# A two-layer graph network on one core: loop with hand-written schedule against an unrolled order by lags

## The chip, the cores and the metric

One core of a Trainium2 chip (trn2) runs the whole program. The metric is the device time of that core in microseconds, the median of several runs.

## What is computed

For 64 graphs of 128 nodes with 128 features (float32) and an integer adjacency matrix of 0 and 1:

```python
e      = leaky_relu((x * a_0) @ x.T, 0.2)           # only adj == 1 occurs in the data
alpha  = softmax(where(adj == 1, e, -9e15), axis=-1)
y      = layernorm(x + alpha @ x)
h      = y @ W_loop.T ;  g = h @ Wg_loop.T
vals   = (h + b_loop) * sigmoid(g + bg_loop)
out    = layernorm(y + relu(adj.T @ vals))
```

Other values of `adj` would take a general path, which is in the program and is skipped here; a sum over `adj` at the end decides that. Sigmoid is written as tanh: 0.5·(tanh(z/2)+1).

## The kernel before, in words

Four graphs make a group, so there are 16 groups of 128 × 512 elements. Five engines each run a list of stages in a fixed order, and semaphores join them. In the order of the data one group g passes through these stages (line numbers in brackets):

- SyncE loads `xt`, `adj_s`, `x_s` of a group (L530 to L532) into one of four slots, and stores `out_s` (L550).
- ScalarE: `weigh` (xat = xt·a, L643), `absent` (1 − adj, with its sum by an accumulator, L631), `mask` (adj as float, L636).
- TensorE `products` (L809: a penalty where there is no edge, L813: the scores, into one of two halves of `p_e`); ScalarE `relu` (L647); VectorE `scores` (L733, four instructions and their maxima); ScalarE `exp` (L654, four, with their sums by an accumulator); TensorE `turn_probs` (L828); ScalarE `turned_probs` (L664); TensorE `attend` (L838); VectorE `inverse` (1/sum, L740), `residual1` (L749, four) and `stats1` (L756, two).
- GpSimd `norm1`: variance + eps (L592), its power −1/2 (L594), and y = res1 · rstd (L596), a 128×512 multiply. This y is not centred; the mean is taken out by centring the weights (`w_mid`).
- TensorE `turn_y` (L847); ScalarE `turned_y` (L668); TensorE `gate_a`, `gate_b`: per half group one bf16 matmul that lays the biases down (L858, operands `ones3` and `b_parts`) and two matmuls of 256 columns (L861); ScalarE `tanh` (L672); VectorE `values` (L762); TensorE `sum_a`, `sum_b` (L872); VectorE `residual2` (L774) and `stats2` (L781).
- GpSimd `norm2`: variance (L602), centring (L613), power −1/2 (L616), multiply into `out_s` (L621). For the last four groups ScalarE does the last step (`finish`, L683).

The table `SCHEDULE` gives each engine a head, a loop body of one turn per group (unrolled four times, in a hardware loop) and a tail. What matters for what follows is the distance between stages on two engines. In one turn of the body VectorE does `residual1:3 scores:4 stats1:3 residual2:1 stats2:1`: it takes the first statistics of a group, and the second ones of the group two before. GpSimd's body is `norm2:2 norm1:5`: the second norm of a group, then the first norm of the group three after. So when GpSimd comes to `norm2` of a group, its `stats2` ended a whole VectorE turn before the `stats1` that the following `norm1` needs.

A `wait_alone` is a wait followed by an instruction that only adds to a semaphore; it stands ahead of L592, L602 and L733.

Of the kernel before, what the change touches and what calls it, by code (L numbers as in the profile page):

```python
# [5 lines left out]
ALU = mybir.AluOpType  # L6
ACT = mybir.ActivationFunctionType
# [10 lines left out]
LATE = 4  # L18
# [8 lines left out]
UNROLL = 4  # L27

SCHEDULE = {
    "tensor": (3, """
        products:0 products:1 turn_probs:0 attend:0 products:2 turn_probs:1 attend:1 products:3 turn_probs:2
        turn_y:0 attend:2 gate_a:0 gate_b:0 turn_y:1 sum_a:0 sum_b:0 gate_a:1 gate_b:1
        """, """
        turn_probs:3 products:4 attend:3 turn_y:2 sum_a:1 sum_b:1 gate_b:2 gate_a:2
        """, """
        turn_probs:15 attend:15 sum_a:13 turn_y:14 sum_b:13 gate_a:14 gate_b:14 sum_a:14 turn_y:15 sum_b:14
        gate_a:15 gate_b:15 sum_a:15 sum_b:15
        """),  # L40
    "scalar": (3, """
        weigh:0 absent:0 relu:0 weigh:1 absent:1 exp:0 relu:1 turned_probs:0 weigh:2 absent:2 exp:1 relu:2
        turned_probs:1 weigh:3 absent:3 exp:2 relu:3 turned_probs:2 mask:0 turned_y:0 mask:1 tanh_a:0
        tanh_b:0 turned_y:1
        """, """
        weigh:4 exp:3 absent:4 turned_probs:3 tanh_b:1 tanh_a:1 mask:2 relu:4 turned_y:2
        """, """
        exp:15 turned_probs:15 tanh_a:13 mask:14 tanh_b:13 turned_y:14 finish:12 tanh_a:14 mask:15 tanh_b:14
        turned_y:15 finish:13 tanh_a:15 tanh_b:15 finish:14 finish:15
        """),  # L50
    "vector": (3, """
        scores:0 inverse:0 scores:1 residual1:0 stats1:0 inverse:1 scores:2 residual1:1 stats1:1
        inverse:2 scores:3 residual1:2 values_a:0 values_b:0 stats1:2 inverse:3
        residual2:0 stats2:0
        """, """
        values_b:1 values_a:1 residual1:3 scores:4 stats1:3 residual2:1 stats2:1 inverse:4
        """, """
        values_a:13 residual1:15 values_b:13 stats1:15 residual2:13 stats2:13 values_a:14 values_b:14 residual2:14 stats2:14 values_a:15 values_b:15 residual2:15
        stats2:15
        """),  # L60
    "gpsimd": (2, """
        norm1:0 norm1:1 norm1:2 norm2:0 norm1:3 norm2:1 norm1:4
        """, """
        norm2:2 norm1:5
        """, """
        norm2:10 norm1:13 norm2:11 norm1:14 norm2:12 norm1:15 norm2:13 norm2:14 norm2:15
        """),
# [3 lines left out]
def program(nc, x, x_t, adj, a_0, a_all, w, wg_t, b_loop, b_fwd, b_bwd, out):  # L71


# [7 lines left out]
    with ExitStack() as ctx:  # L81
# [12 lines left out]
        ones3 = sb("ones3", [3, P], BF16)  # L94
        ones_col = sb("ones_col", [P, 1])
        minus_half = sb("minus_half", [P, G])
        minus_one = sb("minus_one", [P, G])
# [8 lines left out]
        b_rows = sb("b_rows", [3, 2 * P])  # L106
        b_rest = sb("b_rest", [3, 2, 2 * P])
        b_part = sb("b_part", [3, 3, 2 * P], BF16)
        b_sum = sb("b_sum", [3, 2, 2 * P], BF16)
        b_parts = sb("b_parts", [3, 2, 2 * P], BF16)  # L110

        x_s = sb("x_s", [P, 4, G, P])
        adj_s = sb("adj_s", [P, 4, G, P], I32)
        mask = sb("mask", [P, 4, G, P])
        absent = sb("absent", [P, 2, G, P], BF16)


# [40 lines left out]
        x_loaded = [sem(f"x_loaded{i}") for i in range(4)]  # L158
        adj_loaded = [sem(f"adj_loaded{i}") for i in range(4)]
# [4 lines left out]
        b_step = sem("b_step")  # L164
# [6 lines left out]
        xt_loaded = [sem(f"xt_loaded{i}") for i in range(4)]  # L171
# [11 lines left out]
        pool1 = sem("pool1")  # L183
# [17 lines left out]

# [29 lines left out]
        g_bias = [sb(f"g_bias{d}", [P, n, 2 * P]) for d, n in enumerate(n_rel)]  # L231
# [58 lines left out]
        def general_sync(sp):  # L290
# [46 lines left out]
        def general_vector(dve):  # L337
            dve.wait_ge(general_known, 1)
            found = dve.value_load(general[0:1, 0:1], min_val=0, max_val=1)
            with dve.If(found > 0):  # L340
# [7 lines left out]
                with dve.Fori(0, n_graphs) as b:  # L348
# [10 lines left out]
                    nc.vector.tensor_copy(g_xt[:], p_e[:, 1, 0]).then_inc(g_xt_ready, 1)  # L359
                    nc.vector.tensor_copy(g_adjf[:, 1], p_e[:, 1, 1]).then_inc(g_xt_ready, 1)  # L360
# [6 lines left out]
                    nc.vector.tensor_scalar(g_fifth[:], p_e[:, 0], SLOPE, None, ALU.mult).then_inc(g_attn, 1)  # L367
                    own = 2 + 2 * KINDS + 1
                    dve.wait_ge(g_attn, own * b + 1)
                    nc.vector.tensor_tensor(g_leaky[:], p_e[:, 0], g_fifth[:], ALU.max).then_inc(g_attn, 1)  # L370
# [15 lines left out]
                    nc.vector.scalar_tensor_tensor(out=g_res[:], in0=p_o[:, 0], scalar=g_rz[:], in1=g_x[:],  # L386
# [43 lines left out]
        def general_tensor(pe):  # L430
            pe.wait_ge(general_known, 1)
            found = pe.value_load(general[0:1, 0:1], min_val=0, max_val=1)
            with pe.If(found > 0):
# [7 lines left out]
                with pe.Fori(0, n_graphs) as b:  # L441
                    pe.wait_ge(g_loaded, 32 * (b + 1))
                    nc.tensor.transpose(p_e[:, 1, 0], g_x[:], ident[:]).then_inc(g_turned, 1)
                    pe.wait_ge(g_adjf_ready, b + 1)
                    nc.tensor.transpose(p_e[:, 1, 1], g_adjf[:, 0], ident[:]).then_inc(g_turned, 1)
                    pe.wait_ge(g_xa_ready, KINDS * (b + 1))
                    for k in range(KINDS):
                        last = nc.tensor.matmul(p_e[:, 0, k], g_xa[:, k], g_xt[:], start=True, stop=True)
# [4 lines left out]
                    nc.tensor.matmul(p_o[:, 0], g_prob_t[:], g_x[:], start=True, stop=True).then_inc(g_attended, 1)  # L453
# [25 lines left out]
        def is_first(g, n=1):  # L479

            return isinstance(g, int) and g < n

        def is_late(g):

            return isinstance(g, int) and g >= n_groups - LATE

        def of_half(f, h):
            return lambda g, s: f(g, s, h)

        engines = {"tensor": nc.tensor, "scalar": nc.scalar, "vector": nc.vector, "gpsimd": nc.gpsimd}  # L490

        def run(eng, stages):

            turns, head, body, tail = SCHEDULE[eng]

            def do(name, turn=None):
                stage, group = name.split(":")
                g, f = int(group), stages[stage]
                if turn is None:
                    f(g, g % UNROLL)  # L500
                else:
                    f(turn * UNROLL + g, g % UNROLL)

            order = head.split(), body.split(), tail.split()
            names = [n.split(":")[0] for n in order[1]]
            assert sorted(names) == sorted(set(stages) - {"finish"})
            done = list(order[0])
            for name in order[0]:
                do(name)

# [404 lines left out]
```

## Time and profile before

| | us |
|---|---|
| median of 3 runs | 132.62 (131.41 to 133.52) |
| the profiled execution | 132.06 |
| its span, first to last instruction | 130.2 |
| outside the span | 1.86 |

Times in the rows are microseconds from the start of the span, unless ns is written. One f32 matmul leaves two records, and matmul ends are modelled. A duration includes the way through the engine; the next instruction may start some 0.1 us before it ends, so the time an instruction occupies its engine is read from one start to the next.

### The profile page before, as it was taken

Reading aid. Unit: us, or ns where it says so; the run is one execution under the profiler, and the core shown is the slowest. Engines: PE = TensorE matmul, PEld = TensorE weight load, DVE = VectorE, ACT = ScalarE, POOL = GpSimd, SP = SyncE. Lnnn points to the kernel's source line nnn. Section 1 sums busy time; section 2 is a strip of 40 time slices with the busy share of each in tenths; the row PEclk is TensorE's granted clock in tenths of the full one; section 3 lists DMA queues with packets and bytes.
Section 4 is the critical chain, followed back from the end, with each engine's and each line's share of the span. In section 5 each row is a group of like instructions: output and inputs, shape, how many; then the busy total and the mean of one; then the engine's idle time right before and its main releaser. Section 6 shows DMA issues by size and latency. Waiting matters only on the chain.

```text
span 130.2 us, 2906 instructions
## 1 busy us (share of the span) xinstructions
PE 114.8 (88%) x706; PEld 93.9 (72%) x713; DVE 82.9 (64%) x336; ACT 98.8 (76%) x308; POOL 81.4 (63%) x124
## 2 busy tenths in 40 slices
PE   6767778999999999999999999999999997799500
PEld 6757567678878787878787878787878784675400
DVE  0537286635868686868686868686868686756420
ACT  4437899586979797979797979797979785767622
POOL 4000035427678787978797979797979797493340
PEclk9999999999999999999999999999999999999995
DMA  2999500592082656455646465646464202020222
GB/s 54 307 292 290 146 0 0 151 282 61 0 261 61 167 160 182 143 153 172 184 138 181 141 173 149 190 134 189 133 189 133 81 0 81 5 83 0 81 81 83
DMA packets 34768, 17.28 MB, mean 133 GB/s; under 512 B 1219, under 2 KB 34758, under 8 KB 34758
## 3 DMA queue, kind: packets, MB, share of 16 engines
q1 hardware_dynamic: 34608, 17.17, 47.2%
q8 instruction: 3, 0.05, 0.2%
q14 instruction: 7, 0.06, 0.1%
q10 hardware_dynamic: 150, 0.00, 0.1%
HBM read 12.98 MB, written 4.19 MB: 132 GB/s over the span
## 4 chain that ended last, share of the span: by engine, by line
PE 79%; ACT 10%; DMA 3%; issue 3%; DVE 1%; ACTq 0%; SPq 0%; POOL 0%; POOLq 0%; DVEq 0%
PE p_hg L861 26%; PE p_e L813 12%; PE p_ag L872 11%; PE p_o L838 10%; PE p_hg L858 8%; PE p_ut L828 5%; PE p_yt L847 5%; DMA adj_s<-adj 3%; ACT prob L654 2%; ACT absent L631 2%; PE p_e L809 2%; ACT prob_t L664 2%; ACT xat L643 1%; ACT rel L647 1%; ACT out_s L683 1%
## 5 line engine op out<-in xcount | busy, mean ns | idle before, releaser
L861 PE MATMUL p_hg<-w_both,y_t 128*128 128x256 f32 x128 | 36.2, 405 | 0.0
L861 PEld LDWEIGHTS p_hg<-w_both,y_t 128*128 128x128 f32 x128 | 21.7, 189 | 8.9 <-issue 7.3
L762 DVE SCALAR_TENSOR_TENSOR vals<-th,p_hg 128x256 f32<-128x256 f32 x32 | 12.4, 418 | 20.1 <-ACT th L672 20.1
L654 ACT ACTIVATE prob<-nscore,nmax 128x128 f32<-128x128 f32 x64 | 24.7, 389 | 0.4 <-DVE nmax L733 0.4
L592 POOL TENSOR_SCALAR rs<-st 128x4 f32<-128x4 f32 x16 | 3.2, 197 | 33.6 <-DVE st L756 33.6
L749 DVE SCALAR_TENSOR_TENSOR res<-p_o,rz,x_s 128x128 f32<-128x128 f32 x64 | 18.0, 344 | 8.4 <-PE p_o L838 4.3
L838 PE MATMUL p_o<-x_s,prob_t 128*128 128x128 f32 x128 | 17.5, 280 | 2.3 <-ACT prob_t L664 2.3
L813 PE MATMUL p_e<-xt,xat 128*128 128x128 f32 x128 | 18.6, 292 | 0.7 <-ACT absent L631 0.4
L872 PE MATMUL p_ag<-vals,mask 128*128 128x128 f32 x128 | 17.9, 277 | 1.4 <-issue 1.3
L813 PEld LDWEIGHTS p_e<-xt,xat 128*128 128x128 f32 x128 | 18.4, 208 | 0.6
L838 PEld LDWEIGHTS p_o<-x_s,prob_t 128*128 128x128 f32 x128 | 15.5, 192 | 3.3 <-ACT prob_t L664 3.3
L664 ACT ACTIVATE prob_t<-p_ut 128x512 f32<-128x512 f32 x16 | 9.6, 598 | 10.8 <-PE p_ut L828 10.8
L872 PEld LDWEIGHTS p_ag<-vals,mask 128*128 128x128 f32 x128 | 16.0, 191 | 2.3 <-issue 2.0
L596 POOL TENSOR_TENSOR y<-res,rs 128x512 f32<-128x512 f32 x16 | 16.7, 1041 | 1.3
L594 POOL TENSOR_TENSOR rs<-rs,minus_half 128x4 f32<-128x4 f32 x16 | 16.2, 1013 | 1.5 <-POOL rs L592 0.3
L733 DVE CUSTOM_DVE_ANT_0 nscore<-p_e,rel 128x128 f32<-128x128 f32 x64 | 14.7, 285 | 3.1 <-ACT rel L647 2.9
L672 ACT ACTIVATE th<-p_hg 128x256 f32<-128x256 f32 x32 | 10.9, 384 | 4.2 <-PE p_hg L861 4.1
L621 POOL TENSOR_TENSOR out_s<-cent,rs 128x512 f32<-128x512 f32 x12 | 12.5, 1041 | 1.6 <-POOL rs L616 1.0
L668 ACT ACTIVATE y_t<-p_yt 128x512 f32<-128x512 f32 x16 | 9.5, 597 | 4.0 <-PE p_yt L847 4.0
L781 DVE BATCH_NORM_STATS2 st<-res 128x6 f32<-128x256 f32 x32 | 12.2, 424 | 0.6
L613 POOL TENSOR_TENSOR cent<-res,st 128x512 f32<-128x512 f32 x12 | 12.6, 1047 | 0.0
L643 ACT ACTIVATE xat<-xt,a_col 128x512 f32<-128x512 f32 x16 | 11.4, 713 | 1.4 <-DMA xt<-x_t 1.4
(63 smaller groups left out, 182.4 us busy)
## 6 DMA issues: line engine op xcount, KB each, us to landing
xt<-x_t SPq DMA_DIRECT2D x16, 256.0 KB, 3.2
adj_s<-adj SPq DMA_DIRECT2D x16, 256.0 KB, 3.9
x_s<-x SPq DMA_DIRECT2D x16, 256.0 KB, 4.1
out<-out_s SPq DMA_DIRECT2D x15, 256.0 KB, 2.3
out<-out_s SPq DMA_DIRECT2D x2, 128.0 KB, 1.8
w_rows<-w SPq DMA_DIRECT2D x1, 192.0 KB, 4.5
wg_s<-wg_t SPq DMA_DIRECT2D x1, 192.0 KB, 4.8
a_col<-a ACTq DMA_DIRECT2D x1, 0.5 KB, 3.0
```

Of the source, the lines that this page charges most:

```text
L594: nc.gpsimd.tensor_tensor(rs1[:, k, 1], rs1[:, k, 0], minus_half[:], ALU.pow).then_inc(pool1, 1)
L596: nc.gpsimd.tensor_tensor(y[:, s], res1[:, k], rs1[:, k, 1, :, None].broadcast_to([P, G, P]), ALU.mult).then_inc(y_done, 1)
L613: nc.gpsimd.tensor_tensor(cent[:], res2[:, k], st2[:, s, :, 1:2].broadcast_to([P, G, P]), ALU.subtract).then_inc(cent_done, 1)
L621: nc.gpsimd.tensor_tensor(out_s[:, k], cent[:], rs2[:, s, 1, :, None].broadcast_to([P, G, P]), ALU.mult).then_inc(out_done, 1)
L643: nc.scalar.activation(xat[:, s % 2], xt[:, s], ACT.Copy, scale=a_col[:]).then_inc(xat_done, 1)
L654: nc.scalar.activation(prob[:, k, i], nscore[:, k, i], ACT.Exp, scale=-1.0, bias=nmax[:, s, i:i + 1], accum_out=psumz[:, s, i:i + 1]).then ...
L733: nc.vector.tensor_tensor_reduce(nscore[:, k, i], p_e[:, k, i], rel4[:, k, i], -SLOPE, FLOAT_MAX, ALU.add, ALU.min, nmax[:, s, i:i + 1]).t ...
L749: nc.vector.scalar_tensor_tensor(out=res1[:, k, i], in0=p_o[:, i], scalar=rz[:, s, i:i + 1], in1=x_s[:, s, i], op0=ALU.mult, op1=ALU.add). ...
L813: last = nc.tensor.matmul(p_e[:, k, i], xat[:, k, i], xt[:, s, i], start=False, stop=(i == G - 1), skip_group_check=True)
L838: last = nc.tensor.matmul(p_o[:, i], prob_t[:, k, i], x_s[:, s, i], start=True, stop=True)
L861: last = nc.tensor.matmul(p_hg[:, i], y_t[:, k, i], w_both[:], start=False, stop=(i % 2 == 1), skip_group_check=True)
L872: last = nc.tensor.matmul(p_ag[:, i], mask[:, s, i], vals[:, k, i], start=True, stop=True)
```

## The change

The program is written out without loops. `ORDER` gives each engine one list of stages with a lag: in turn n the engine does each stage for group n − lag, in the order of the list. There are 19 turns with work on VectorE and TensorE (0 to 18). Beside this:

- All inputs have their own place in SBUF, and loads run up to five groups ahead of the products. `x_s` has a 129th column of ones per graph; `attend` multiplies 129 columns and leaves the softmax sum in `p_o[:, :, :, P]`. `exp` has no accumulator any more, and the reciprocal reads `p_o` and sits in `residual1`.
- `absent` and `mask` are made for two groups by one ScalarE instruction of 1024 elements, in every second turn.
- The biases are added once to `w_both` (a matmul by a row of 1/128), `turned_y` adds 1 to y, and the bf16 bias matmuls go.
- y is centred and scaled on VectorE (`centre`, four instructions per group); GpSimd's `norm1` ends with the power.
- `norm2` writes `out_s` in two halves, for every group; `finish` is gone.
- `p_e` is one tile: `products` of a group waits for all `scores` of the group before.
- `wait_alone` is gone from these stages.

```diff
+ORDER = {
+    "tensor": "turn_probs:1 products:0 attend:1 turn_y:2 sums:3 gates:2",
+    "scalar": "tanhs:3 turned_probs:1 weigh:-1 relu:0 absent:-1 mask:2 turned_y:2 exp:0",
+    "vector": "values:3 centre:2 scores:0 residual1:1 stats1:1 residual2:3 stats2:3",
+    "gpsimd": "norm2:3 norm1:1",
+    "sync": "load:-5 store:5",
+}
...
+            for turn in range(min(lags), n_groups + max(lags)):
+                for name, lag in steps:
+                    if 0 <= turn - lag < n_groups:
+                        stages[name](turn - lag)
...
             def norm1(g):
-                wait_alone(nc.gpsimd, st1_done, 2 * (g + 1))
+                pool.wait_ge(st1_done, 2 * (g + 1))
...
-                nc.gpsimd.tensor_tensor(y[:, s], res1[:, k], rs1[:, k, 1, :, None].broadcast_to([P, G, P]),
-                                        ALU.mult).then_inc(y_done, 1)
...
             def norm2(g):
+                pool.wait_ge(st2_done, 2 * (g + 1))
...
+                for h in range(2):
+                    nc.gpsimd.tensor_tensor(out_s[:, k, half(h)], cent[:, half(h)],
+                                            rs2[:, k, 1, half(h), None].broadcast_to([P, G // 2, P]),
+                                            ALU.mult).then_inc(out_done, 1)
...
             def residual1(g):
+                dve.wait_ge(av_done, g + 1)
+                nc.vector.reciprocal(rz[:, k].rearrange("p (a b) -> p a b", a=2), p_o[:, :, :, P]).then_inc(rz_done, 1)
+                dve.wait_ge(rz_done, g + 1)
...
+            def centre(g):
+                dve.wait_ge(rstd1_done, g + 1)
+                dve.wait_ge(st1_done, 2 * (g + 1))
...
+                for i in range(G):
+                    nc.vector.tensor_scalar(y[:, g % 4, i], res1[:, k, i], st1[:, k, i, 1:2], rs1[:, k, 1, i:i + 1],
+                                            ALU.subtract, ALU.mult).then_inc(y_done, 1)
...
             def products(g):
+                if g >= 1:
+                    pe.wait_ge(score_done, G * g)
...
             def gates(g):
-                nc.tensor.matmul(p_hg[:, half(h)], ones3[:], b_parts[:], start=True, stop=False,
-                                 skip_group_check=True)
...
             def evac_yt(g):
-                nc.scalar.activation(y_t[:, s % 2], p_yt[:], ACT.Copy).then_inc(yt_done, 1)
+                nc.scalar.activation(y_t[:, g % 2], p_yt[:], ACT.Copy, bias=1.0).then_inc(yt_done, 1)
```

How the instructions now stand on two engines. First GpSimd before, in the head of its list: L592, L594, L596 are `norm1` of group 3, the rest `norm2` of group 1.

```order
L592 TENSOR_SCALAR rs<-st 128x4 [waits st1_done]
L594 TENSOR_TENSOR rs<-rs,minus_half 128x4 [waits pool1]
L596 TENSOR_TENSOR y<-res,rs 128x512 [waits pool1]
L602 TENSOR_SCALAR rs<-st 128x4 [waits st2_done]
L613 TENSOR_TENSOR cent<-res,st 128x512 [waits out_done]
L616 TENSOR_TENSOR rs<-rs,minus_half 128x4 [waits pool2]
L621 TENSOR_TENSOR out_s<-cent,rs 128x512 [waits cent_done,pool2]
```

The same engine after, one turn of the middle: `norm2` of group 2 (L516 to L529), then `norm1` of group 4 (L506, L511).

```order
L516 TENSOR_SCALAR rs<-st 128x4 [waits st2_done]
L520 TENSOR_TENSOR cent<-res,st 128x512 [waits out_done]
L523 TENSOR_TENSOR rs<-rs,minus_half 128x4 [waits var2_done]
L529 TENSOR_TENSOR out_s<-cent,rs 128x256 [waits stored0,rstd2_done,cent_done]
L529 TENSOR_TENSOR out_s<-cent,rs 128x256
L506 TENSOR_SCALAR rs<-st 128x4 [waits st1_done]
L511 TENSOR_TENSOR rs<-rs,minus_half 128x4 [waits y_done,var1_done]
```

The 128×512 multiply by rstd left this engine. Both norms stand in every turn; `norm2` of a group now is followed by `norm1` of the group two after it, where the loop had three.

VectorE before, at the end of its head: `residual1:2`, `values:0`, `stats1:2`, `inverse:3`, `residual2:0`, `stats2:0`.

```order
L749 SCALAR_TENSOR_TENSOR res<-p_o,rz,x_s 128x128 x3
L762 SCALAR_TENSOR_TENSOR vals<-th,p_hg 128x256 [waits tanh_done0]
L762 SCALAR_TENSOR_TENSOR vals<-th,p_hg 128x256 [waits tanh_done1]
L756 BN_STATS st<-res 128x6 [waits r1_done] x2
L740 RECIPROCAL rz<-psumz 128x4 [waits exp_done]
L774 SCALAR_TENSOR_TENSOR res<-p_ag,y 128x512 [waits ag_done1,ag_done0]
L781 BN_STATS st<-res 128x6 [waits r2_done]
```

VectorE after, from the end of turn 3 into turn 4: `residual1:2`, `stats1:2`, `residual2:0`, `stats2:0`, then `values:1`, `centre:2` and the first of `scores:4`.

```order
L658 SCALAR_TENSOR_TENSOR res<-p_o,rz,inputs 128x128 x3
L666 BN_STATS st<-res 128x6 [waits r1_done] x2
L696 SCALAR_TENSOR_TENSOR res<-p_ag,y 128x512 [waits y_done,ag_done1,ag_done0]
L703 BN_STATS st<-res 128x6 [waits r2_done]
L703 BN_STATS st<-res 128x6
L686 SCALAR_TENSOR_TENSOR vals<-th,p_hg 128x256 [waits tanh_done0]
L686 SCALAR_TENSOR_TENSOR vals<-th,p_hg 128x256 [waits tanh_done1]
L677 TENSOR_SCALAR y<-res,st,rs 128x128 [waits st1_done,rstd1_done]
L677 TENSOR_SCALAR y<-res,st,rs 128x128 x3
L645 ISA nscore,nmax<-p_e,rel 128x128 [waits exp_done,rel4_done]
```

L677 is new on this engine and waits for GpSimd's L511 (`rstd1_done`); before, no instruction here waited for GpSimd's result of the same norm.

## Rows read from the trace of the kernel before

**Rows 1.** The page: busy time of the engines, GB/s by slice, chain by engine.
```profile
PE 114.8 (88%) x706; PEld 93.9 (72%) x713; DVE 82.9 (64%) x336; ACT 98.8 (76%) x308; POOL 81.4 (63%) x124
...
GB/s 54 307 292 290 146 0 0 151 282 61 0 261 61 167 160 182 143 153 172 184 138 181 141 173 149 190 134 189 133 189 133 81 0 81 5 83 0 81 81 83
...
PE 79%; ACT 10%; DMA 3%; issue 3%; DVE 1%; ACTq 0%; SPq 0%; POOL 0%; POOLq 0%; DVEq 0%
```

**Rows 2.** Windows, the body and one turn: length, busy by engine, PEclk, DMA share, GB/s.
```profile
31.40:109.80 78.40, 78.13 (x510) 64.45 (x514) 57.91 (x240) 66.06 (x213) 64.30 (x84) 1.00 0.49 141
...
60.90:67.42 6.52, 6.52 (x45) 5.38 (x44) 4.83 (x21) 5.60 (x19) 5.48 (x8) 1.00 0.55 161
```

**Rows 3.** Timeline of TensorE, one turn: start, duration.
```profile
60.83 0.38 PE L858 MATMUL p_hg<-b_parts,ones 3*128 3x512 bf16 x1
61.15 1.13 PE L861 MATMUL p_hg<-w_both,y_t 128*128 128x256 f32 x4
62.21 0.39 PE L858 MATMUL p_hg<-b_parts,ones 3*128 3x512 bf16 x1
...
65.93 0.60 PE L847 MATMUL p_yt<-ident,y 128*128 128x128 f32 x4
66.37 1.06 PE L872 MATMUL p_ag<-vals,mask 128*128 128x128 f32 x8
67.36 0.38 PE L858 MATMUL p_hg<-b_parts,ones 3*128 3x512 bf16 x1
```

**Rows 4.** Timeline of GpSimd: one norm2 and the norm1 behind it.
```profile
64.89 0.20 POOL L602 TENSOR_SCALAR rs<-st 128x4 f32<-128x4 f32 x1
65.05 1.05 POOL L613 TENSOR_TENSOR cent<-res,st 128x512 f32<-128x512 f32 x1
66.06 1.01 POOL L616 TENSOR_TENSOR rs<-rs,minus_half 128x4 f32<-128x4 f32 x1
67.14 1.04 POOL L621 TENSOR_TENSOR out_s<-cent,rs 128x512 f32<-128x512 f32 x1
69.04 0.20 POOL L592 TENSOR_SCALAR rs<-st 128x4 f32<-128x4 f32 x1 [0.85 <-DVE st L756]
69.32 1.01 POOL L594 TENSOR_TENSOR rs<-rs,minus_half 128x4 f32<-128x4 f32 x1
```

**Rows 5.** Timeline of VectorE, one turn without its values.
```profile
66.20 1.13 DVE L749 SCALAR_TENSOR_TENSOR res<-p_o,rz,x_s 128x128 f32<-128x128 f32 x4 [0.41 <-issue]
67.24 0.28 DVE L733 CUSTOM_DVE_ANT_0 nscore<-p_e,rel 128x128 f32<-128x128 f32 x1
...
68.08 0.76 DVE L756 BATCH_NORM_STATS2 st<-res 128x6 f32<-128x256 f32 x2
68.76 0.67 DVE L774 SCALAR_TENSOR_TENSOR res<-p_ag,y 128x512 f32<-128x512 f32 x1
69.47 0.76 DVE L781 BATCH_NORM_STATS2 st<-res 128x6 f32<-128x256 f32 x2
70.15 0.16 DVE L740 RECIPROCAL rz<-psumz 128x4 f32<-128x4 f32 x1
```

**Rows 6.** Groups by line: busy us, mean ns; then idle time ahead.
```profile
L716 DVE TENSOR_SCALAR w_mid<-w_rows,w_mean 128x128 f32<-128x128 f32 x1 | 0.3, 286 | 0.0
...
L701 DVE COPY b_rest<-b_rows 3x128 f32<-3x128 f32 x1 | 0.2, 206 | 0.0
```

**Rows 7.** Waits of GpSimd for the second statistics: us in total, times, longest.
```profile
POOL rs L602 <- DVE st L781: 5.9, 3, 2.9
```

**Rows 8.** Timeline of GpSimd: the first norm2 of the run.
```profile
31.54 0.20 POOL L602 TENSOR_SCALAR rs<-st 128x4 f32<-128x4 f32 x1 [0.86 <-DVE st L781]
```

**Rows 9.** Timeline, the end: ScalarE's last output, 128x128 four times.
```profile
126.27 1.65 ACT L683 ACTIVATE out_s<-res,shift,rs 128x128 f32<-128x128 f32 x4 [2.82 <-POOL shift L609]
```

**Rows 10.** Timeline of TensorE: the first products, eight records of 128x128.
```profile
6.76 1.91 PE L813 MATMUL p_e<-xt,xat 128*128 128x128 f32 x8
```

**Rows 11.** Window at the end of the run, columns as in rows 2.
```profile
124.00:130.20 6.20, 0.19 (x2) 0.09 (x2) 0.69 (x4) 1.65 (x4) 1.51 (x4) 0.72 0.30 86
```

More of the change, by code:

```diff
@@ L25 @@
 FLOAT_MAX = 3.0e38
[L27 to L67, printed above, removed]
+AHEAD = 5
+ORDER = {
[4 more added lines that the diff above has]
+    "sync": "load:-5 store:5",
 }
@@ L477, in half @@
             return slice(h * G // 2, (h + 1) * G // 2)
[L479 to L490, printed above, removed]
-        def run(eng, stages):
[L494 to L509, printed above, removed]
-            with engines[eng].Fori(0, turns) as turn:
-                for u in range(UNROLL):
-                    for name in order[1]:
-                        stage, k = name.split(":")
-                        do(f"{stage}:{int(k) + u}", turn)
-                        done += [f"{stage}:{int(k) + u + UNROLL * i}" for i in range(turns)]
-            for name in order[2]:
-                do(name)
-            done += order[2]
-            done = [name for name in done if not name.startswith("finish:")]
-            assert sorted(done) == sorted(f"{x}:{g}" for x in names for g in range(n_groups))
@@ L670, in tanh @@
[L670 to L684 removed]
+                if g >= 2:
+                    act.wait_ge(hg_done[1], g - 1)
@@ new lines, in values @@
+            def values(g):
+                k = g % 2
+                for h in range(2):
+                    dve.wait_ge(tanh_done[h], g + 1)
+                    if g >= 2:
+                        dve.wait_ge(ag_done[h], g - 1)
+                    nc.vector.scalar_tensor_tensor(out=vals[:, k, half(h)], in0=th[:, k, half(h)], scalar=1.0,
+                                                   in1=p_hg[:, half(h), 0], op0=ALU.add, op1=ALU.mult)\
+                        .then_inc(vals_done[h], 1)
@@ L788, in _ @@
-            dve.wait_ge(mask_done, n_groups)
+            run("vector", {"scores": scores, "residual1": residual1, "stats1": stats1, "centre": centre,
+                           "values": values, "residual2": residual2, "stats2": stats2})
+            dve.wait_ge(mask_done, n_pairs)
+            dve.wait_ge(const_done, 7)
             nc.vector.tensor_reduce(sum_rows[:], sums[:], AX_XY, ALU.add).then_inc(sum_done, 1)
             dve.wait_ge(sum_done, 2)
-            nc.vector.tensor_scalar(general[:], p_e[0:1, 0, 0, 0:1], float(x.shape[0] * P * P), None,
+            nc.vector.tensor_scalar(general[:], p_e[0:1, 0, 0:1], float(x.shape[0] * P * P), None,
@@ L865, in neighbours @@
[L865 to L878 removed]
+                for h in range(2):
+                    if g >= 1:
+                        pe.wait_ge(vals_done[h], g)
+                    for i in range(2 * h, 2 * h + 2):
+                        last = nc.tensor.matmul(p_hg[:, i], y_t[:, g % 2, i], w_both[:], start=True, stop=True)
+                    last.then_inc(hg_done[h], 1)
@@ new lines, in neighbours @@
+            def neighbours(g):
+                s = g % 4
+                if g >= 1:
+                    pe.wait_ge(r2_done, g)
+                pe.wait_ge(mask_done, g // 2 + 1)
+                for h in range(2):
+                    pe.wait_ge(vals_done[h], g + 1)
+                    for i in range(2 * h, 2 * h + 2):
+                        last = nc.tensor.matmul(p_ag[:, i], mask[:, s * G + i], vals[:, g % 2, i], start=True, stop=True)
+                    last.then_inc(ag_done[h], 1)
+            run("tensor", {"turn_probs": transpose_u, "turn_y": transpose_y, "products": products, "attend": attend,
+                           "gates": gates, "sums": neighbours})
```

494 lines of the change are left out of this document (226 added, 268 removed).

## The prediction

> **What bounds the kernel now.** I read the page first: TensorE is busy 88% of the span, ScalarE 76%, and the chain that ended last is TensorE for 79% [rows 1]. The average hides fill and drain, so the windows come next: from 31.4 to 109.8 TensorE is busy 78.13 of 78.40 us, and one turn of 6.52 us has 6.52 us of it, beside 4.83 of VectorE, 5.60 of ScalarE and 5.48 of GpSimd [rows 2]. So in the body nothing but TensorE's own work sets the pace, and every other engine has about a microsecond to spare per turn. In the timeline of that turn, from bias matmul to bias matmul 60.83 to 67.36 [rows 3], each bias matmul takes 61.15 − 60.83 = 0.32 us. GpSimd waits for second statistics only 3 times, 5.9 us in all [rows 7]: the loop between VectorE and GpSimd is slack before.
>
> **What the change takes from TensorE.** Two bias matmuls per turn go: 0.64 us, so 6.53 − 0.64 = 5.89 us per turn. `attend` grows by one column in 128 (under 0.01 us). If TensorE still set the pace this would be worth 16 × 0.64 = 10 us. ScalarE loses four accumulator reads and half of two; by its 5.60 it stays below TensorE. DMA ran at a share of 0.49 in the body [rows 2] and the bytes are the same; the earlier loads lie in a fill that already ran near 290 GB/s [rows 1]. I put both at nothing in the body, covered by the wait that follows.
>
> **What the change adds: a loop of VectorE and GpSimd, one lap per turn.** VectorE's turn n does `values(n−3) centre(n−2) scores(n) residual1(n−1) stats1(n−1) residual2(n−3) stats2(n−3)`. GpSimd's turn n does `norm2(n−3)`, then `norm1(n−1)`. `norm2(n−3)` waits for `stats2(n−3)`, the last thing VectorE does in turn n. Behind it in GpSimd's queue stands `norm1(n−1)`, whose statistics were ready long before. And `centre(n−1)`, second in VectorE's turn n+1, waits for that `norm1(n−1)`, with `scores`, `residual1` and both statistics of the turn queued behind it. So from turn 3 to turn 16 neither engine can work while the other does (only `values`, 0.7 us, lies beside GpSimd's part). The price of a turn is the sum of the two parts.
>
> VectorE, from rstd to the last `stats2`:
> - `residual1, scores, stats1, residual2, stats2`: one unbroken stretch from 66.20 to 69.47 + 0.76 = 70.23, 4.03 us [rows 5].
> - `centre`: four TENSOR_SCALAR 128×128. L716 is the one row of that form, 0.286 us [rows 6]. Four `scores` take 68.08 − 67.24 = 0.84, 0.21 each at a duration of 0.28 [rows 5], so I take 4 × 0.21 = 0.84.
> - the reciprocal, now on the path with a wait behind it: 0.16 [rows 5], 0.20 with the hand-over.
> - Sum 5.07 us.
>
> GpSimd, from its variance to the next rstd:
> - `norm2`: 64.89 to 67.14 + 1.04 = 68.18, 3.29 us [rows 4]. The last multiply is now two of half the size: one more fixed part, which I take as most of the 0.20 of a four-element instruction [rows 4], less what overlaps: 0.12 (between 0 and 0.20).
> - `norm1` without its multiply: 69.04 to 69.32 + 1.01 = 70.33, 1.29 us [rows 4].
> - Sum 4.70 us.
>
> Hand-overs: VectorE's first statistics end at 68.08 + 0.76 = 68.84 and GpSimd starts at 69.04, 0.20 later [rows 4, 5], with a `wait_alone` between that now goes; I take 0.08 for it, and 0.05 for the way back. **A turn is then 5.07 + 4.70 + 0.13 = 9.9 us**, 3.4 more than the 6.52 of before.
>
> **Is something else later still?** Count from the rstd. `turn_y` (66.37 − 65.93 = 0.44), then `sums` (67.36 − 66.37 = 0.99) [rows 3] are released by `centre` and done some 2 us after it began; VectorE reaches `residual2` after 0.84 + 0.84 + 0.20 + 1.04 + 0.68 = 3.6 us. `products` and `relu` for the next turn lie in the wait. The one score tile makes `products` wait for `scores` of the turn before, which ended 8 us earlier: nothing. TensorE has 9.9 − 5.9 = 4.0 us idle per turn, VectorE about 4.1, in one piece in front of `centre`.
>
> **The sum.** Before, the first `norm2` starts at 31.54 [rows 8]. On the way there were four bias matmuls of groups 0 and 1 (1.3 us), which go: 30.5 for the first `norm2`, in turn 3. From there:
> - `norm2` of groups 0 to 12, twelve laps: 12 × 9.9 = 118.8, so 149.3.
> - turn 16 has no `scores` (−0.84): 9.1, so 158.4.
> - turn 17 has `centre(15)` behind GpSimd's 4.7, then `turn_y`, `sums`, `residual2` and `stats2` in a row, about 0.3 + 0.7 + 1.1 + 0.7 + 0.8 = 3.6 and hand-overs: 8.5, so 166.9.
> - turn 18 is gates, tanh, values, sums, residual2 and stats2 of group 15, of which the gates began in turn 17: 3.7, so 170.6.
> - the last `norm2`, 3.4: 174.0. Before, the last output was ready at 126.27 + 1.65 = 127.92 of 130.2 [rows 9], 2.3 us before the end: 176.3.
> - Outside the span 1.86 us as before: **178 us**. The sum is against the profiled execution, 132.06; the median of the runs is 132.62, 0.6 higher, which is within what I can claim.
>
> So the 10 us taken from TensorE are never seen: they become idle time, and 13 laps × 3.4 = 44 us come on top, with small terms of both signs at the ends.
>
> **A rule weighed against the trace: two elements per cycle.** L716, an f32 tensor_scalar within SBUF with a per-partition scalar, took 286 ns for 128 columns, and the plain copy L701 of 128 columns 206 ns [rows 6]. The copy ran 80 ns shorter at the same number of columns. The Trainium skill, "VectorE: DVE Perf Modes" (section "Mode 2×_2P — use both read ports for one tensor"), says that single-source f32 operations within SBUF get two elements per cycle, tensor_scalar among them; by it the four `centre` instructions would be nearer to the copy, 0.13 each. I take the row of the same form. By the copy's price a turn is 0.3 us shorter and the time 174.
>
> **The rivals.**
> *A. TensorE falls to its lower clock and becomes the bound (7%).* In the window 124.0 to 130.2, where TensorE works 0.19 us, the mean granted clock is 0.72 [rows 11]: it fell from 2.4 to 1.2 GHz after the matmuls had ended. The first products took 1.91 us for eight records, the same number in the body 1.06 [rows 10, 3]. In the new turn TensorE stands still for some 3.6 us in one piece, longer than any gap in the body now, shorter than the last one. At half clock its turn is 2 × 5.89 = 11.8 us, over the 9.9 of the loop: 1.9 × 13 turns = 24, and some 8 at both ends: 210 us. Against it: while it is slow it would be busy all the time, which should bring the clock back. Losses that only fill its 4 us of slack cost nothing; a mixture costs 0 to 8 us and lies in my range. The Trainium skill, "TensorE: Matmul & The Clock Gate" (section "HAM oscillation — how this bites in real kernels"), describes matmul kernels that drop to half clock in every iteration behind a wait; by it rival A, or the mixture, would be the likely case.
>
> *B. The loop has a lap of two turns, not one (5%).* If `norm2(n−3)` met statistics that are already there, GpSimd's 4.7 us and VectorE's 5.8 would lie beside TensorE's 5.9, and TensorE would set the pace again, at 5.9 to 6.1 with VectorE close behind. Then 13 turns save 0.45 each: 132.06 − 6 = 126 us, faster by 4.6%. It decides where `stats2` of the same group stands in VectorE's list: one turn earlier and B is right. The loop of before is made that way, as rows 7 show by its few waits. Against B is the order of the instructions: the first turn with `norm2` has `stats2` of that very group at VectorE's end.
>
> *C. A wait that I don't see adds to the lap (2%).* ScalarE's exps or a store in front of the half multiplies: over 189 us.
>
> **How the numbers follow.** The forecast, a lap of 9.9 us at mostly full clock, has 86%. Its bounds per lap: 9.5 (centre at the copy's price, no cost of halves) is 172; 10.5 (two pointer scalars dearer than L716, 0.30 each, the halves 0.20, hand-overs of 0.2) is 186, and up to 3 more for a clock that falls now and then. Range 171 to 189. Slower by over 2%: forecast, A and C, 0.95. Faster 0.04 and within 2% 0.01 come from B, since 126 has room on both sides. Within 2% is what a measurement of this kernel cannot tell from no change.
>
> **What would show it.** Right: GpSimd's L516 waits for VectorE's L703 in nearly every turn, some 5 us each; VectorE's L677 waits for GpSimd's L511 about 4 us each, 13 or 14 times; turns of 9.9 us; TensorE busy below 65%; the chain split between VectorE and GpSimd. L677 at 0.21 from start to start confirms the `centre` term, 0.13 the skill's rule. Wrong: a turn near 6 us (B), TensorE without gaps and products at 1.9 us (A), or a wait of L677 that ends with another engine (C).

## The result and the profile after

185.16 us (median of 4 runs, 184.56 to 185.83) against 133.03 for the kernel before beside it: ratio 1.403, interval 1.388 to 1.417. The profiled execution took 185.56 us, 183.8 of it span. The forecast was 178, range 171 to 189. Medians and ranges here are of all executions, while a ratio, always against the kernel before run beside it, compares only those in the faster of the two states in which a program can run.

The page after, busy time by engine, and the waits (engine, line waited for: us in total, times, longest):

```profile
PE 127.4 (69%) x684; PEld 111.8 (61%) x684; DVE 97.3 (53%) x390; ACT 86.8 (47%) x198; POOL 73.8 (40%) x125
```
```profile
POOL rs L516 <- DVE st L703: 81.2, 16, 5.5
DVE y L677 <- POOL rs L511: 54.3, 16, 4.2
ACT y_t L606 <- PE p_yt L772: 49.2, 15, 5.2
PEld p_yt L772 <- issue: 43.1, 14, 4.8
PE p_yt L772 <- DVE y L677: 40.9, 15, 4.4
```

No engine is busy 70%. GpSimd waited for second statistics 3 times before [rows 7]; now it does so in all 16 groups, 5.1 us each on average, and VectorE's `centre` waits for GpSimd's power (L511), 3.4 us each. These two waits point at each other. TensorE and ScalarE wait too, but behind `centre`. The page's chain of work ends after 1% here, so the loop has to be read from the waits and from the timelines of the two engines, one turn of the middle each, VectorE first, to be set beside [rows 4, 5]:

```profile
87.56 1.12 DVE L677 TENSOR_SCALAR y<-res,st,rs 128x128 f32<-128x128 f32 x4 [3.85 <-POOL rs L511]
88.59 0.28 DVE L645 CUSTOM_DVE_ANT_0 nscore<-p_e,rel 128x128 f32<-128x128 f32 x1
...
89.44 0.18 DVE L653 RECIPROCAL rz<-p_o 128x4 f32<-128x4 f32 x1
89.65 1.13 DVE L658 SCALAR_TENSOR_TENSOR res<-p_o,rz,inputs 128x128 f32<-128x128 f32 x4
90.69 0.76 DVE L666 BATCH_NORM_STATS2 st<-res 128x6 f32<-128x256 f32 x2
91.36 0.68 DVE L696 SCALAR_TENSOR_TENSOR res<-p_ag,y 128x512 f32<-128x512 f32 x1
92.07 0.77 DVE L703 BATCH_NORM_STATS2 st<-res 128x6 f32<-128x256 f32 x2
...
97.70 1.11 DVE L677 TENSOR_SCALAR y<-res,st,rs 128x128 f32<-128x128 f32 x4 [3.80 <-POOL rs L511]
```
```profile
82.79 0.19 POOL L516 TENSOR_SCALAR rs<-st 128x4 f32<-128x4 f32 x1 [5.40 <-DVE st L703]
82.94 1.04 POOL L520 TENSOR_TENSOR cent<-res,st 128x512 f32<-128x512 f32 x1
83.95 1.01 POOL L523 TENSOR_TENSOR rs<-rs,minus_half 128x4 f32<-128x4 f32 x1
85.09 1.18 POOL L529 TENSOR_TENSOR out_s<-cent,rs 128x256 f32<-128x256 f32 x2
86.24 0.19 POOL L506 TENSOR_SCALAR rs<-st 128x4 f32<-128x4 f32 x1
86.51 1.01 POOL L511 TENSOR_TENSOR rs<-rs,minus_half 128x4 f32<-128x4 f32 x1
92.93 0.19 POOL L516 TENSOR_SCALAR rs<-st 128x4 f32<-128x4 f32 x1 [5.40 <-DVE st L703]
```

GpSimd works from 82.79 to 87.52; VectorE starts `centre` at 87.56 and ends its statistics at 92.84; GpSimd starts again at 92.93. The engines take turns, and a turn is 92.93 − 82.79 = 10.14 us. TensorE in the same turn:

```profile
84.22 1.06 PE L763 MATMUL p_o<-inputs,prob_t 128*128 128x129 f32 x8
88.05 1.15 PE L772 MATMUL p_yt<-ident,y 128*128 128x128 f32 x4 [2.78 <-DVE y L677]
89.00 1.92 PE L794 MATMUL p_ag<-vals,mask 128*128 128x128 f32 x8
```
```profile
89.00:91.00 2.00, 2.00 (x10) 2.00 (x10) 1.96 (x12) 1.76 (x5) 0.00 (x0) 0.50 0.27 80
92.90:97.90 5.00, 2.56 (x22) 2.33 (x20) 0.88 (x3) 3.12 (x6) 4.52 (x7) 1.00 0.10 32
```

The two windows have their columns as in [rows 2]. TensorE stands still for 2.8 us in front of `turn_y` (L772). In the window behind that wait the granted clock is 0.50, that is 1.2 GHz, and `sums` (L794) take 1.92 us in place of 1.06 [rows 3]; in the window 92.90 to 97.90 it is 2.4 GHz again. `sums` take 1.91 to 1.93 us in every turn from 4 to 17.

One margin is thin. `sums` end at 89.00 + 1.92 = 90.92, and `residual2` (L696), which needs them, starts at 91.36: 0.44 us later.

### The profile page after: what moved, and what is told of

The parts are those of the page before. It is cut to its first block and busy times, and to the rows that moved or that the text cites. A ratio compares the mean times of both kernels' runs of the same rounds, so it can differ in the third digit from the quotient of the medians.

```text
span 183.8 us, 2563 instructions
## 1 busy us (share of the span) xinstructions
PE 127.4 (69%) x684; PEld 111.8 (61%) x684; DVE 97.3 (53%) x390; ACT 86.8 (47%) x198; POOL 73.8 (40%) x125
## 5 line engine op out<-in xcount | busy, mean ns | idle before, releaser
L677 DVE TENSOR_SCALAR y<-res,st,rs 128x128 f32<-128x128 f32 x64 | 17.9, 343 | 54.3 <-POOL rs L511 54.3
L772 PE MATMUL p_yt<-ident,y 128*128 128x128 f32 x64 | 17.7, 397 | 40.9 <-DVE y L677 40.9
L772 PEld LDWEIGHTS p_yt<-ident,y 128*128 128x128 f32 x64 | 10.4, 163 | 46.9 <-issue 43.1
L516 POOL TENSOR_SCALAR rs<-st 128x4 f32<-128x4 f32 x16 | 3.1, 194 | 81.2 <-DVE st L703 81.2
L794 PE MATMUL p_ag<-vals,mask 128*128 128x128 f32 x128 | 29.3, 404 | 0.3 <-DVE vals L686 0.3
L794 PEld LDWEIGHTS p_ag<-vals,mask 128*128 128x128 f32 x128 | 27.3, 313 | 0.8 <-DVE vals L686 0.5
L529 POOL TENSOR_TENSOR out_s<-cent,rs 128x256 f32<-128x256 f32 x32 | 18.9, 612 | 2.1
L658 DVE SCALAR_TENSOR_TENSOR res<-p_o,rz,inputs 128x128 f32<-128x128 f32 x64 | 18.0, 345 | 0.6
L734 PEld LDWEIGHTS p_e<-inputs,xat 128*128 128x128 f32 x128 | 17.7, 200 | 0.7
L734 PE MATMUL p_e<-inputs,xat 128*128 128x128 f32 x128 | 17.7, 284 | 0.0
L763 PE MATMUL p_o<-inputs,prob_t 128*128 128x129 f32 x128 | 17.2, 277 | 0.7 <-ACT prob_t L600 0.7
L511 POOL TENSOR_TENSOR rs<-rs,minus_half 128x4 f32<-128x4 f32 x16 | 16.2, 1013 | 1.3
L763 PEld LDWEIGHTS p_o<-inputs,prob_t 128*128 128x128 f32 x128 | 15.9, 194 | 0.9 <-ACT prob_t L600 0.9
L523 POOL TENSOR_TENSOR rs<-rs,minus_half 128x4 f32<-128x4 f32 x16 | 16.1, 1007 | 0.0
```

The source lines that it names most:

```text
L511: nc.gpsimd.tensor_tensor(rs1[:, k, 1], rs1[:, k, 0], minus_half[:], ALU.pow).then_inc(rstd1_done, 1)
L523: nc.gpsimd.tensor_tensor(rs2[:, k, 1], rs2[:, k, 0], minus_half[:], ALU.pow).then_inc(rstd2_done, 1)
L529: nc.gpsimd.tensor_tensor(out_s[:, k, half(h)], cent[:, half(h)], rs2[:, k, 1, half(h), None].broadcast_to([P, G // 2, P]), ALU.mult).then ...
L658: nc.vector.scalar_tensor_tensor(out=res1[:, k, i], in0=p_o[:, i // 2, i % 2, 0:P], scalar=rz[:, k, i:i + 1], in1=x_s(g)[:, i, 0:P], op0=A ...
L677: nc.vector.tensor_scalar(y[:, g % 4, i], res1[:, k, i], st1[:, k, i, 1:2], rs1[:, k, 1, i:i + 1], ALU.subtract, ALU.mult).then_inc(y_done, 1)
L734: last = nc.tensor.matmul(p_e[:, i], xat[:, k, i], xt(g)[:, i], start=False, stop=(i == G - 1), skip_group_check=True)
```

## The experiments

The theory to be tested, T: each turn is one lap through VectorE's `stats2`, GpSimd's `norm2` and `norm1`, and VectorE's `centre`. Its rivals: L, TensorE's lower clock sets the turn; S, the single score tile and the shallow buffers do. The turn of a run is the mean of twelve laps, from one start of `norm2` to the next.

**Break the lap: exchange the two stages.**

```diff
-    "gpsimd": "norm2:3 norm1:1",
+    "gpsimd": "norm1:1 norm2:3",
```

> The changed kernel with one line exchanged: GpSimd does norm1 of a group before the norm2 that stands in the same turn. Theory T (one lap per turn through VectorE's stats2, GpSimd's norm2 and norm1, VectorE's centre): norm1 then waits only for stats1, the lap is broken, TensorE sets the pace again at 5.9 to 6.1 us per turn in place of 10.13, and the time is 127 us (124 to 130). Rival L (TensorE's lower clock behind each wait sets the turn): the order of two GpSimd stages frees little work on TensorE; the turn stays over 8 us and the time over 160. Rival S (one score tile and two-deep buffers join the engines too tightly): the turn stays near 10 us, about 180.

131.16 us (129.24 to 132.72), ratio 0.991 (0.985 to 0.997). One exchange took 54 us off, with the single score tile and the buffers as they were: S falls. The turn is 6.29 us, not 5.9 to 6.1, and the time is outside my range of 124 to 130.

**Break it the other way: norm2 one turn later.**

```diff
-    "gpsimd": "norm2:3 norm1:1",
+    "gpsimd": "norm2:4 norm1:1",
```

> The changed kernel with norm2 one turn later on GpSimd (lag 4 in place of 3), still ahead of norm1. Theory T: norm2 then meets statistics that ended with the turn before, so its 3.5 us run at the turn's start beside other work, as in the loop of the kernel before: the same 127 us as with the two stages exchanged, within 2 us, perhaps 1 more at the end since the last norm2 comes no later than its statistics. Rivals L and S: no more than a few us off the changed kernel's 185.

129.44 us (two executions), ratio 0.984 (0.977 to 0.991), turn 6.30. Nothing was done for TensorE, and its clock is at 1.00 from 30 to 110 us once nobody waits. That alone does not refute L, since lap and clock changed together; the filler below separates them. This version is the base of the later ones.

**Put a known price on the lap.**

```diff
+                nc.gpsimd.tensor_tensor(spare[:], rs1[:, k, 0], minus_half[:], ALU.pow).then_inc(spared, 1)
```

> The changed kernel with norm1's power done twice, the first one into a spare tile: 1.01 us more of GpSimd in each of 16 groups. Theory T: it lies on the lap, so each of the 14 turns that have norm2 and norm1 of turn 3 to 16 costs the whole 1.01 us: turn 11.15, time 185.2 + 14 = 199 (197 to 202). Rival L or S: GpSimd is busy 40% of the span, so another 16 us of it hide; time within 3 us of 185.

201.7 us, 16.5 more than the changed kernel. In the trace twelve laps go from 34.00 to 167.27, 11.11 each, 0.97 longer by a power of 1.01. GpSimd was busy 40% of the span, and still next to nothing of its added 16 us hid. I had counted 14 groups and left out the two in the fill, where the first `norm2` comes 1.9 us later.

**Work for TensorE in its gap.**

```diff
+                for i in range(12 if g >= 1 else 0):
+                    nc.tensor.matmul(p_yt[:, i % 4], warm[:], warm[:], start=True, stop=True).then_inc(warmed, 1)
```

> The changed kernel with 12 extra matmuls of 128x128 on a tile of zeros per group, in front of turn_y, where TensorE stands still for 2.8 to 3.6 us; 2.7 us at full pace. They keep the array at work. Theory T: the turn stays 10.13 us, turn_y and sums go from 1.15 and 1.92 us back to 0.60 and 1.06, and only the last two turns, where TensorE is on the path, gain: 182.5 us (180 to 185). Rival L: the slow matmuls are on the path of each turn, and 12 turns gain up to 1.5 us each: 167 to 175. If the filler itself runs at half clock or delays turn_y, the time rises instead, up to 15 turns of 2 us.

185.86 us, just outside the range of 180 to 185. TensorE in one turn:

```profile
85.65 2.84 PE L771 MATMUL p_yt<-warm 128*128 128x128 f32 x24
89.73 1.10 PE L774 MATMUL p_yt<-ident,y 128*128 128x128 f32 x4 [1.24 <-DVE y L677]
90.66 1.06 PE L796 MATMUL p_ag<-vals,mask 128*128 128x128 f32 x8
```

`sums` are back at 1.06 us, the granted clock from 40 to 150 us is 1.00 in place of 0.84, and the turn is 10.13 as before. So L falls: the lower clock cost the lap nothing, nor did 15 × 2.8 us of extra matmuls. `turn_y` stays at 1.10; it waits for each of the four `centre` instructions, which I had taken for the clock. In total nothing was gained: the filler made the first `norm2` 1.75 us later (33.88), and the last turns gave back 1.4.

**Why 6.30 and not 5.9?** VectorE is busy all the time in the versions without the lap. With norm2 one turn later, `centre` reads

```profile
64.10 1.57 DVE L677 TENSOR_SCALAR y<-res,st,rs 128x128 f32<-128x128 f32 x4
```

1.57 us against 1.12 above, where GpSimd stood still. Theory P of the expectations says that `centre` and GpSimd's 128×512 instructions hinder each other. Three runs take this apart. Leave out the multiplication by rstd (the scale is missing from y), so that each instruction has one per-partition scalar:

```diff
...
-st1[:, k, i, 1:2], rs1[:, k, 1, i:i + 1], ALU.subtract, ALU.mult)
+st1[:, k, i, 1:2], None, ALU.subtract)
...
```

> On the version with norm2 one turn later: centre subtracts the mean and leaves out the multiplication by rstd, so it has one per-partition scalar in place of two; the output is another one. In that version the four centre instructions take 1.57 us, against 1.11 us in the changed kernel, where GpSimd stands still beside them. Theory P (they and GpSimd's 128x512 operations hinder each other): the count of scalars does not matter, centre stays at 1.5 us or more and the time at 129.4 within 0.7. Rival N (the second scalar is what makes centre dearer than the 0.84 of my sum): centre falls by 0.2 us or more per turn, the time to 127 or less.

127.55 us (two executions); `centre` 1.40, turn 6.12. Neither forecast was met, and both theories have a part: the second scalar costs 0.04 us per instruction, and the rest of the excess stays. Let `norm2` treat 4 of 128 columns (the rest of the output is zero):

```diff
-nc.gpsimd.tensor_tensor(cent[:], res2[:, k], st2[:, k, :, 1:2].broadcast_to([P, G, P]),
+nc.gpsimd.tensor_tensor(cent[:, :, 0:4], res2[:, k, :, 0:4], st2[:, k, :, 1:2].broadcast_to([P, G, 4]),
... (the same for the two multiplies into out_s)
```

> On the version with norm2 one turn later: norm2 treats 4 of 128 columns of each graph (the rest of the output is zero), with all its waits and instructions kept. Theory P: GpSimd no longer reads and writes beside centre, whose four instructions fall from 1.57 to 1.11 us as in the changed kernel; the turn goes from 6.30 to 5.9 (TensorE's own 5.89 is the floor), 13 turns x 0.4 = 5 us, and the last norm2 is shorter by some 2 us: 122.5 us (121 to 124.5). Rival N: centre stays at 1.5 us, the turn at 6.30, and only the 2 us of the last norm2 are gained: 127.4.

122.64 us (two executions), `centre` 1.10, turn 5.84: as theory P says. Write `centre` as scalar_tensor_tensor:

```diff
+nc.vector.scalar_tensor_tensor(out=y[:, g % 4, i], in0=res1[:, k, i], scalar=st1[:, k, i, 1:2],
+                               in1=rs1[:, k, 1, i:i + 1].broadcast_to([P, P]), ...)
```

> On the version with norm2 one turn later: centre is written as scalar_tensor_tensor, the rstd as a broadcast second tensor, in place of tensor_scalar with two scalars. The same form with one operand in PSUM takes 0.26 us from start to start (residual1). Theory P1 (only tensor_scalar, with a single source in SBUF, shares something with GpSimd): 4 x 0.26 = 1.04 in place of 1.50, turn 5.9, 124 us (123 to 126). Rival P2 (any VectorE instruction that reads two operands from SBUF meets GpSimd just so): 1.5 us or more, and 129.4 or more.

130.39 us, ratio 0.988 (0.979 to 0.998), `centre` 1.65: P2, it is not the form of the instruction. Then take GpSimd's power ahead of its centring, so that the centring starts later:

```diff
-                nc.gpsimd.tensor_tensor(cent[:], res2[:, k], st2[:, k, :, 1:2].broadcast_to([P, G, P]),
-                                        ALU.subtract).then_inc(cent_done, 1)
                 pool.wait_ge(var2_done, g + 1)
                 nc.gpsimd.tensor_tensor(rs2[:, k, 1], rs2[:, k, 0], minus_half[:], ALU.pow).then_inc(rstd2_done, 1)
+                nc.gpsimd.tensor_tensor(cent[:], res2[:, k], st2[:, k, :, 1:2].broadcast_to([P, G, P]),
+                                        ALU.subtract).then_inc(cent_done, 1)
```

> On the version with norm2 one turn later: GpSimd's norm2 takes the power of the variance (four elements, 1.01 us) ahead of the centring of 512 columns, not behind it. The centring then starts 1.1 us later, when VectorE's four centre instructions are nearly through. Theory P (VectorE's instructions with operands in SBUF alone are held up while GpSimd streams 512 columns, and not by the power on four): centre goes from 1.49 us to 1.15, the turn from 6.30 to 5.95, 13 turns x 0.35 = 4.5 us: 125 us (123.5 to 126.5). Rival Q (centre is held up by any work of GpSimd beside it): centre stays at 1.4 us or more, the time at 129.4 within 1.

134.42 us, ratio 1.014 (1.006 to 1.022), turn 6.63: the opposite of what I expected. By its time alone it would speak for Q, so the instructions have to be read one by one. The timeline, VectorE and GpSimd:

```profile
65.82 1.90 DVE L677 TENSOR_SCALAR y<-res,st,rs 128x128 f32<-128x128 f32 x4
```
```profile
65.62 1.09 POOL L519 TENSOR_TENSOR rs<-rs,minus_half 128x4 f32<-128x4 f32 x1
66.60 1.04 POOL L522 TENSOR_TENSOR cent<-res,st 128x512 f32<-128x512 f32 x1
67.72 1.18 POOL L529 TENSOR_TENSOR out_s<-cent,rs 128x256 f32<-128x256 f32 x2
```

Looked at one by one, three of the four start at 65.82, 66.08 and 66.34 and take 0.34; the fourth starts at 66.6, with the centring, and takes 1.13, to 67.73, where the centring ends at 67.64. In the base version it is the first one that is long, and GpSimd's centring ends at 64.83:

```profile
64.10 0.80 DVE L677 TENSOR_SCALAR y<-res,st,rs 128x128 f32<-128x128 f32 x1
```
```profile
63.78 1.05 POOL L520 TENSOR_TENSOR cent<-res,st 128x512 f32<-128x512 f32 x1
64.78 1.01 POOL L523 TENSOR_TENSOR rs<-rs,minus_half 128x4 f32<-128x4 f32 x1
```

So a single instruction is held until the 128×512 one has ended, and the power on four elements holds none: P is right, Q is not, and what I had wrong was the moment at which the centring comes. GpSimd's centring takes 1.04 to 1.05 us in either case. My shift had moved the collision from the centring's last part to its whole.

**Ends of the run.** Weight loads earlier (behind group 0's), on the base version:

```diff
-                if g == 1:
+                if g == 0:
                     sp.dma_start(w_rows[:], w.rearrange("k f d -> f k d")).then_inc(w_loaded, 16)
```

> On the version with norm2 one turn later (129.4 us, turn 6.30 us, VectorE busy nearly all of it): the two weight loads are issued behind group 0's three loads in place of group 1's. Theory F (the fill lost 1.6 us because the weight mix, on TensorE ahead of products of group 1, waits 3.3 us for w_mid): w_mid then follows scores of group 0 directly, some 0.7 us earlier, and the run ends 0.7 to 1.5 us earlier: 128.3. Rival: group 1's own inputs, now 0.4 MB later, take over as the last to arrive, and nothing is gained or 1 us is lost: 129.4 to 130.5.

129.68 us (128.89 to 132.03): the rival, no gain. The first `norm2` came at 32.53, against 32.14, and TensorE still waited 3.6 us for `w_mid`. On the power-first version, the last group's output on VectorE:

```diff
+                if g == n_groups - 1:
...
+                    for i in range(G):
+                        done = nc.vector.tensor_scalar(out_s[:, k, i], res2[:, k, i], st2[:, k, i, 1:2],
+                                                       rs2[:, k, 1, i:i + 1], ALU.subtract, ALU.mult)
... (GpSimd's norm2 of the last group ends with the power)
```

> The version before, and for the last group the output is centred and scaled on VectorE (four instructions) behind GpSimd's power, in place of GpSimd's centring and two multiplies. At the end of the run nothing lies beside it: after the last statistics 0.28 + 1.01 + 1.1 = 2.4 us to the last output in place of 3.5: 1 us less than the version before (0.5 to 1.3), 124 us.

132.52 us against 134.42 without it, run beside it. From the last variance to the end of the last output it is 126.91 + 1.11 − 125.59 = 2.4 us in place of 3.6, 1.1 us less, as expected. The rest is in the fill: the first `norm2` starts at 31.34 against 32.20, 0.9 us apart without a reason in the code. On top of it, the fill in another order:

```diff
             def attend(g):
+                if g == 0:
+                    mix_weights()
...
+                for of in {0: [], 1: [0], 2: [], 3: [1, 2, 3]}.get(g, [g]):
+                    sp.dma_start(x_s(of)[:, :, 0:P], x_v[of]).then_inc(x_loaded[of], 16)
... (on ScalarE the copies of w_both move from turned_probs to turned_y of group 0)
```

> The version before, and in the fill: products of group 1 ahead of the weight mix on TensorE, the copies of w_both behind on ScalarE, and x_s of groups 0 to 3 loaded behind the adj_s that absent of the pair 2 and 3 waits for. Theory F2 (the first norm2 comes at 32.1 us because products of group 1 wait for the mix, 3.3 us, and then absent for the pair for its loads): the first norm2 comes 1.5 to 3 us earlier and so does the end: 122 us. Rival: the chain of exp, turn_probs, attend and the first norms holds the fill, and the gain is under 0.7 us.

132.01 us (130.70 to 132.32), against 132.52 (132.36 to 132.56) without it. The first `norm2` comes at 29.49 in place of 31.34, and the span is 128.8 in place of 130.7: in these two traces F2's 1.9 us. But this trace is of the fastest execution, and the spans of the other three are 130.1 to 130.5. The medians show 0.5. Seven traces with the old fill have their first `norm2` at 31.3 to 32.2, and the two with the new one (this and the last run below) at 29.5 and 30.3. So the new order is earlier, but by how much is left open, and so is the share of each of its two parts.

**Wait on purpose.**

```diff
+                pool.wait_ge(y_done, G * min(g + 3, n_groups))
                 nc.gpsimd.tensor_tensor(cent[:], res2[:, k], st2[:, k, :, 1:2].broadcast_to([P, G, P]),
```

> The version before, with one wait more: GpSimd starts its centring of 512 columns only when VectorE's centre of the same turn is done. In the traces of the last versions one of the four centre instructions stands still exactly while GpSimd's 128x512 centring runs (it started at 66.60 beside it at 66.60 and took 1.13 us, the three before it 0.34), and none beside the power on four elements. Theory P3 (a VectorE instruction with operands in SBUF alone and a GpSimd instruction that streams 512 columns exclude each other, and the later one waits): all four take 0.34 again, centre 1.1 us, the turn goes from 6.63 to 5.9, 13 turns x 0.7 = 9 us: 122.5 us (121 to 124.5), 7% under the kernel before. Rival (the centring, started later, holds up another VectorE instruction or makes norm1 and with it the next centre late): a turn of 6.3 or more, 128 us or more.

120.07 us (118.25 to 121.60), ratio 0.893 (0.884 to 0.901): better than expected and 10.7% under the kernel before. VectorE and GpSimd:

```profile
63.08 0.76 DVE L670 BATCH_NORM_STATS2 st<-res 128x6 f32<-128x256 f32 x2
...
65.79 1.11 DVE L681 TENSOR_SCALAR y<-res,st,rs 128x128 f32<-128x128 f32 x4
```
```profile
61.21 1.04 POOL L526 TENSOR_TENSOR cent<-res,st 128x512 f32<-128x512 f32 x1 [0.36 <-DVE y L681]
62.33 1.18 POOL L533 TENSOR_TENSOR out_s<-cent,rs 128x256 f32<-128x256 f32 x2
...
67.05 1.05 POOL L526 TENSOR_TENSOR cent<-res,st 128x512 f32<-128x512 f32 x1 [0.36 <-DVE y L681]
```
```profile
30.00:100.00 70.00, 69.62 (x492) 63.24 (x490) 69.16 (x289) 61.38 (x142) 56.55 (x85) 1.00 0.39 115
```

GpSimd waits 0.36 us, VectorE gets its 0.8 us back, and the turn is 67.05 − 61.21 = 5.84. Between the traces of the last two runs twelve laps are 9.5 us shorter and the last turns 1.5. TensorE and VectorE are both busy 99% of the body. By the sum the two bias matmuls taken from TensorE count here for the first time: with their 0.64 us its turn would be near 6.5, as before. No run puts them back.

## Why the prediction was right, point by point

- **The lap, one per turn.** This was the mechanism forecast, and it is shown: by breaking it in two ways, by its price (the second power), and by the filler. That it lasts from turn 3 on is in the trace: 12 laps from 32.13 to 153.72, 10.13 each.
- **Its size, 9.9.** 10.13. GpSimd's part was 4.73 (term 4.70), the hand-overs 0.04 and 0.09 (0.13 together, as taken). VectorE's was 5.28, not 5.07: `centre` takes 0.257 from start to start, not 0.21. I took the row with one per-partition scalar and the new instruction has two; the run without the scale shows the difference. Twelve laps: 2.8 us.
- **The rule of two elements per cycle.** By it, as the prediction takes it from the Trainium skill, "VectorE: DVE Perf Modes" (section "Mode 2×_2P — use both read ports for one tensor"), its estimate was 0.13 per `centre` instruction; 0.257 was measured. In its effect on time the trace is against it here: `residual1`, with two tensor inputs, has the same 0.26 from start to start. How much of the 0.257 is columns and how much is the fixed part of an instruction no run shows.
- **Fill, 30.5 for the first norm2.** 32.13. The step that failed is the credit of 1.3 us for the bias matmuls (the sum has it as 1.0: 31.54 − 1.3 is 30.2). `products` of group 1 now stands behind the weight mix on TensorE, which waited 3.3 us for `w_mid`. I had not looked at this order. Putting it right, with the loads, gave 1.9 us between two traces and less between the medians.
- **Turns 16 to 18 and the end.** 9.71, 9.79 and 4.38 in place of 9.1, 8.5 and 3.7: together 2.6 us. Without `scores` and `residual1` as cover VectorE waits for `sums` in turns 17 and 18, 3.2 us together. In turn 17:

```profile
168.19 1.12 DVE L677 TENSOR_SCALAR y<-res,st,rs 128x128 f32<-128x128 f32 x4 [3.05 <-POOL rs L511]
171.64 0.69 DVE L696 SCALAR_TENSOR_TENSOR res<-p_ag,y 128x512 f32<-128x512 f32 x1 [2.33 <-PE p_ag L794]
```
```profile
169.63 1.92 PE L794 MATMUL p_ag<-vals,mask 128*128 128x128 f32 x8
171.34 2.95 PE L783 MATMUL p_hg<-w_both,y_t 128*128 128x256 f32 x8
```

  The lower clock adds 0.86 us to `sums` there and stretches the gates of the last group to 2.95 us, from 1.94 at full clock in the filler run. This is rival A's clock, small and only where TensorE is on the path. The last `norm2` and store took 0.5 more than put down. All terms: 1.6 + 2.8 + 2.6 + 0.5 = 7.5, from 176.3 to 183.8.
- **Rival A.** The clock fell in every turn from 4 to 17, as the rule in the Trainium skill, "TensorE: Matmul & The Clock Gate" (section "HAM oscillation — how this bites in real kernels"), lets one expect, and in the lap it did not bind: this is the mixture that rival A prices at 0 to 8 us. TensorE was slow for part of a turn only. The prediction took its 4 us of idle as what decides, but that is the sum over a turn. What decides is whether `sums` are there when VectorE comes to `residual2`, and there I was lucky: I had them done some 2 us after `centre` began. They ended 90.92 − 87.56 = 3.4 us after it (2.4 at full clock, in the filler run), and `residual2` began 3.8 us after it. The step "done some 2 us after" failed; 0.44 us more on TensorE, and the clock would have cost something in each turn.
- **Rival B.** Wrong for the kernel as it stands, right as a recipe: with the lap broken the time is 129 to 131. The turn of 5.9 to 6.1 in it left out what VectorE loses to GpSimd, 6.30 against 5.84 in the run where `norm2` treats 4 columns. No row of before could show this: GpSimd made y itself there.

## What to carry to other kernels

Where two engines work in fixed orders and hand results both ways, write down for one turn which item of the one stands behind which of the other; if the way round closes within a turn, the two busy times add up however idle both look. One place in a list decided 54 us here, more than every instruction saved. And a wait can be worth its time: 0.36 us of waiting on an engine with slack saved 0.8 us on the engine that had none.

## What I had not expected of the hardware

A `centre` instruction, whose tensors lie in SBUF alone (tensor_scalar, and as well scalar_tensor_tensor with both inputs in SBUF), did not finish while GpSimd's 128×512 TENSOR_TENSOR ran: 1.13 us in place of 0.34 when both started together, and 0.80 when it met the rest. GpSimd's own instruction kept its 1.04 to 1.05 us. Its power on four elements held nobody, but took 1.09 us itself where `centre` ran beside it as in the power-first version, against 1.01; why, no run shows. `scores` and `residual1`, with one operand in PSUM, kept 0.28 and 0.34 us in the last version, where GpSimd's centring and multiplies lie beside them. The statistics, which read one SBUF tensor, kept 0.76 us for two from 63.08 on, beside a multiply that ran to 63.51. The Trainium skill, "GPSIMD Engine Reference" (section "1. Specifications"), says that the two engines share SBUF interfaces and contend where VectorE runs in a two-port mode or with two SBUF inputs; for the form with two SBUF inputs the runs agree. That tensor_scalar was held too fits, but whether it ran in such a mode no run shows. The loss in these runs is the whole rest of GpSimd's instruction.
